# Context attention with its heads in two row halves, a pair of maxima per slot, and values weighed every second slot

## The reference, cut to what matters

```python
# ctx_512: 4 x 4096 x 128; HEADS = 16, D_K = 16
qh = (layernorm(x) @ Wq + bq)   # 4 batches x 16 heads x 256 queries x 16
kh = (ctx_512 @ Wk + bk)        # 4 batches x 16 heads x 4096 keys x 16
vh = (ctx_512 @ Wv + bv)
scores = einsum('bhqd,bhkd->bhqk', qh, kh) / 4
out = softmax(scores) @ vh
x = x + out @ Wo + bo
```

## Time and profile before

| | |
|---|---|
| times of three runs | 1427.91, 1429.73, 1433.0 us; median 1429.73 |
| span of the profiled execution | 1429.1 us, 0.6 below the median; no time around the span is shown |
| slot 0 begins, last slot begins | 67.1 us, 963 us |
| busy share PE, DVE, ACT, POOL | 96%, 74%, 65%, 20% |
| mean granted clock of PE | 0.989; 1.00 in all of the slots |

### The profile page before, as it was taken

How to read it: one execution, slowest core, us unless ns; L and a number is a source line. 1 busy time by engine, 2 the same in 40 slices (tenths; PEclk the granted TensorE clock), 3 DMA queues, 4 the chain that set the end, 5 groups by cost and what they waited for, 6 DMA issues and landing times.

```text
span 1429.1 us, 28070 instructions
## 1 busy us (share of the span) xinstructions
PE 1375.6 (96%) x11138; PEld 846.7 (59%) x11138; DVE 1055.1 (74%) x2114; ACT 922.1 (65%) x1899; POOL 287.6 (20%) x321
## 2 busy tenths in 40 slices
PE   7799999999999999999999999999999999989998
PEld 5355555555555545555554556556557999856666
DVE  4787777787777778777778888835876778767757
ACT  5366777767777767777767666672796664448731
POOL 3354222222222222122213100000003100001210
PEclk9899999999999999999999999999999999999999
DMA  6966555346554545655454743002402320347000
GB/s 184 163 145 143 119 118 111 77 102 130 116 127 92 102 84 125 128 115 113 81 97 101 184 73 61 2 1 60 119 18 65 112 67 1 91 112 155 2 1 30
DMA packets 95587, 133.19 MB, mean 93 GB/s; under 512 B 8864, under 2 KB 70944, under 8 KB 89504
## 3 DMA queue, kind: packets, MB, share of 16 engines
q1 hardware_dynamic: 95456, 131.40, 42.3%
HBM read 94.15 MB, written 37.22 MB: 92 GB/s over the span
## 4 chain that ended last, share of the span: by engine, by line
PE 79%; ACT 8%; DVE 8%; DMA 2%; issue 2%; SPq 1%; POOL 0%; DVEq 0%; ACTq 0%
PE psum L559 16%; PE psum L540 13%; PE psum L524 13%; ACT probs L783 4%; PE psum L2132 4%; PE psum L587 3%; PE psum L2106 3%; DVE peaks L685 3%; PE psum L626 3%; PE psum L1226 2%; PE psum L2851 2%; PE psum L1623 1%; PE psum L275 1%; PE psum L2861 1%; PE psum L2814 1%
## 5 line engine op out<-in xcount | busy, mean ns | idle before, releaser
L685 DVE TENSOR_REDUCE peaks<-psum 128x1 f32<-128x512 f32 x1024 | 643.3, 684 | 197.0 <-PE psum L524 196.4
L783 ACT ACTIVATE probs<-psum 128x512 f32<-128x512 f32 x1024 | 529.0, 615 | 83.3 <-PE psum L540 79.4
L524 PE MATMUL psum<-keysT,queriesT 96*128 96x512 bf16 x1024 | 390.1, 384 | 13.2 <-DMA keysT<-key_parts 7.9
L540 PE MATMUL psum<-queriesT,keysT 98*128 98x256 bf16 x2048 | 392.4, 274 | 6.1 <-ACT queriesT L846 2.4
L540 PEld LDWEIGHTS psum<-queriesT,keysT 98*128 98x128 bf16 x2048 | 176.3, 99 | 191.7 <-ACT probs L783 72.1
L559 PE MATMUL psum<-probs,values 128*17 128x256 f32 x4096 | 245.9, 380 | 0.0
L559 PEld LDWEIGHTS psum<-probs,values 128*17 128x17 f32 x4096 | 107.2, 97 | 102.6 <-issue 27.1
L524 PEld LDWEIGHTS psum<-keysT,queriesT 96*128 96x128 bf16 x1024 | 98.6, 96 | 90.9 <-issue 56.1
L918 POOL CAST key_parts<-key_f 128x512 bf16<-128x512 f32 x57 | 34.8, 611 | 518.0 <-ACT key_f L816 511.0
L816 ACT ACTIVATE key_f<-psum,bk 128x512 f32<-128x512 f32 x59 | 40.5, 687 | 120.7 <-PE psum L587 120.6
L587 PE MATMUL psum<-ctxT,wk 128*128 128x512 f32 x128 | 69.5, 625 | 2.4 <-DVE probs L728 0.9
(11 more groups left out here) (315 smaller groups left out, 1662.5 us busy)
## 6 DMA issues: line engine op xcount, KB each, us to landing
keysT<-key_parts SPq DMA_DIRECT2D x31, 768.0 KB, 7.7
key_parts<-key_parts SPq DMA_DIRECT2D x90, 256.0 KB
keysT<-key_parts SPq DMA_DIRECT2D x31, 512.0 KB, 10.1
ctx_nat<-in_ctx_dram SPq DMA_DIRECT2D x32, 256.0 KB, 3.0
keysT<-key_parts SPq DMA_DIRECT2D x31, 256.0 KB, 11.6
ctx_in<-in_ctx_dram SPq DMA_DIRECT2D x24, 256.0 KB, 5.9
ctx_turned<-ctxT SPq DMA_DIRECT2D x24, 256.0 KB, 4.4
ctx_T<-ctx_turned SPq DMA_DIRECT2D x12, 512.0 KB, 3.8
```

What stands on the lines that cost most here:

```text
L524: e.matmul(ps, self.queriesT[0:ROWS, u % 2, g * GH + j, t * P:(t + 1) * P], self.keysT[0:ROWS, i % RING, j, c * BANK:(c + 1) * BANK], star ...
L540: made = e.matmul(ps[:, j * S:(j + 1) * S], self.keysT[0:AUG, i % RING, j, kt * P:(kt + 1) * P], self.queriesT[0:AUG, u % 2, g * GH + j, : ...
L685: e.tensor_reduce(self.peaks[:, i % 2, pair, c:c + 1], k.ps(("max", n)), AX.X, ALU.max).then_inc(*self.peaked.up(n))
L783: e.activation(self.probs[:, t % RINGP, e2 * GH * S:(e2 + 1) * GH * S], k.ps(("scores", t, e2)), ACT.Exp).then_inc(*self.exped.up((t, e2)))
```

## The change

Three things change, all in the first block.

1. The two heads of a group stand in two row halves of the array: head 0 in partitions 0 to 63, head 1 in 64 to 127. `keysT` and `queriesT` get two planes: `MAIN` with four of the six products (64 rows), and `REST` with the other two and the two rows of the maximum (34 rows). A score is two matmuls in a row, one of each plane, that add up; a slot has eight of 256 columns instead of four. Each head has a bank for the whole slot, shared by both key tiles, so ACT's exponentials are one for each head and not one for each key tile. The maxima are taken over the four products of `MAIN` alone, one matmul for each head, and both stand behind the slot's scores.
2. The values are weighed every second slot (`BLOCK` = 2), after the maxima.
3. Value projections of a batch come every eighth slot (the last four more closely), and the jobs on even slots, the weighings on odd ones.

With it go six DMAs instead of three where keys are read (of 32 partitions each, the same bytes), four instead of three for query rows, five instead of three for a batch's query parts, and two copies of the maximum's rows on ACT instead of one.

```diff
-HALVES, SUMS = 3, 3
+SCORES, SUMS, BLOCK = (0, 1, 2), 3, 2
...
-        self.keysT = sb(scope, "keysT", [P, RING, GH, LC], BF16)
+        self.keysT = sb(scope, "keysT", [P, 2, RING, LC], BF16)
...
-                slot = UNIT * u - 101 + 8 * c
+                slot = UNIT * u - 100 + 8 * c
...
-                at(SLOTS * NG * b - 97 + 6 * p, "make values", b, p)
+                at(SLOTS * NG * b + (8 * p - 96 if p < 12 else (-6, 0, 2, 8)[p - 12]), "make values", b, p)
...
-            e.matmul(ps, self.queriesT[0:ROWS, u % 2, g * GH + j, t * P:(t + 1) * P],
-                     self.keysT[0:ROWS, i % RING, j, c * BANK:(c + 1) * BANK],
-                     start=True, stop=True).then_inc(*self.max_made.up(n))
+            e.matmul(ps, self.queriesT[own, MAIN, u % 2, g, qt * P:(qt + 1) * P],
+                     self.keysT[own, MAIN, i % RING, c * BANK:(c + 1) * BANK],
+                     start=True, stop=True).then_inc(*self.max_made[j].up(n))
...
-            for e2 in range(2):
-                if 0 <= t < TOTAL:
-                    kt, n = 2 * p + e2, (2 * t + e2) % HALVES
-                    ps = banks.use(n, w, ("scores", t, e2), (self.exped, (t, e2)))
-                    for j in range(GH):
-                        made = e.matmul(ps[:, j * S:(j + 1) * S], self.keysT[0:AUG, i % RING, j, kt * P:(kt + 1) * P],
-                                        self.queriesT[0:AUG, u % 2, g * GH + j, :], start=True, stop=True)
-                    made.then_inc(*self.scored.up((t, e2)))
-                if maxima and not e2:
-                    find_max(maxima[0], t)
-            if t % 4 == 1 and 5 <= t <= TOTAL + 1:
-                i, p0 = divmod(t - 5, SLOTS)
+                ps = {}
+                for e2 in range(2):
+                    kt = 2 * p + e2
+                    for plane, rows in ((MAIN, HALF), (REST, TALL)):
+                        for j in range(GH):
+                            if j not in ps:
+                                ps[j] = banks.use(SCORES[(2 * t + j) % len(SCORES)], w, ("scores", t, j), (self.exped, (t, j)))
+                            own = slice(j * HALF, j * HALF + rows)
+                            made = e.matmul(ps[j][:, e2 * S:(e2 + 1) * S], self.keysT[own, plane, i % RING, kt * P:(kt + 1) * P],
+                                            self.queriesT[own, plane, u % 2, g, :], start=(plane == MAIN), stop=(plane == REST))
+                            if e2 and plane == REST:
+                                made.then_inc(*self.scored[j].up((t, j)))
+            for n in maxima:
+                find_max(n, t)
+            if (t - 1) % BLOCK == 0 and BLOCK + 1 <= t <= TOTAL + 1:
+                i, p0 = divmod(t - BLOCK - 1, SLOTS)
...
-            for n in maxima[1:]:
-                find_max(n, t)
...
-                for e2 in range(2):
-                    w.wait_ge(self.scored, (t, e2))
-                    e.activation(self.probs[:, t % RINGP, e2 * GH * S:(e2 + 1) * GH * S], k.ps(("scores", t, e2)),
-                                 ACT.Exp).then_inc(*self.exped.up((t, e2)))
+                for j in range(GH):
+                    w.wait_ge(self.scored[j], (t, j))
+                    e.activation(self.probs[:, t % RINGP, 2 * j * S:(2 * j + 2) * S], k.ps(("scores", t, j)),
+                                 ACT.Exp).then_inc(*self.exped.up((t, j)))
...
-        for block, run in RUNS:
-            e.dma_start(self.keysT[block * DH:(block + run) * DH, i % RING, :, keys],
-                        self.key_dram[u, g * GH:(g + 1) * GH, PARTS - run:PARTS, :, keys].rearrange(
-                            "j i d n -> (i d) j n")).then_inc(*landed.up(key))
+        for j in range(GH):
+            for row, plane, first in ((0, MAIN, 1), (LOW, MAIN, 1), (0, REST, 0)):
+                e.dma_start(self.keysT[j * HALF + row:j * HALF + row + LOW, plane, i % RING, keys],
+                            self.key_dram[u, g * GH + j, first:first + 2, :, keys].rearrange("i d n -> (i d) n")).then_inc(
+                    *landed.up(key))
```

More of the change, by code:

```diff
@@ L297 @@
 RUNS = ((0, 3), (3, 2), (5, 1))
-PAIRS = 6
-ROWS = PAIRS * DH
-AUG = ROWS + 2
+KEY_AT = (1, 2, 0)
+QUERY_AT = ((2, 3), (0, 1), (4,))
+HALF = P // 2
+MAIN, REST = 0, 1
+LOW = 2 * DH
+TALL = LOW + 2
 NG = H // GH
@@ L512, in find_max @@
         def find_max(n, now):
-            i, r = divmod(n, MAXES)
-            pair, c = self.max_at(n)
-            j, t = divmod(pair, QT)
+            i, j, qt, c = self.max_at(n)
             u, g = divmod(i, UNIT_GROUPS)
+            own = slice(j * HALF, (j + 1) * HALF)
             job, let_go = ("max", n), (self.peaked, n)
@@ L978, in sync @@
                     n, first, last = CONST_COLS["ones"]
-                    for r in range(ROWS, AUG):
-                        e.dma_start(self.keysT[r:r + 1, :, :, :].rearrange("o r h n -> o (r h n)").bitcast(F32).rearrange(
-                            "o (p n) -> o p n", p=P), io["const"][:, first:last].unsqueeze(0)).then_inc(*self.ones_in.up(0))
+                    for r in (LOW, LOW + 1, HALF + LOW, HALF + LOW + 1):
+                        e.dma_start(self.keysT[r:r + 1, REST, :, :].rearrange("o r n -> o (r n)").bitcast(F32).rearrange(
+                            "o (p n) -> o p n", p=P), io["const"][:, first:(first + last) // 2].unsqueeze(0)).then_inc(
+                            *self.ones_in.up(0))
                 elif job == "load x":
@@ L989, in sync @@
                     if i >= RING:
-                        w.wait_ge(self.scored, (SLOTS * (i - RING + 1) - 1, 1))
+                        for j in range(GH):
+                            w.wait_ge(self.scored[j], (SLOTS * (i - RING + 1) - 1, j))
                     self.read_keys(e, i, slice(0, LC), self.keys_here[i % RING], i)
@@ L1002, in sync @@
                     if u >= 2:
-                        w.wait_ge(self.scored, (UNIT * (u - 1) - 1, 1))
-                    for block, run in RUNS:
-                        e.dma_start(self.queriesT[block * DH:(block + run) * DH, u % 2, :, :],
-                                    self.q_dram[b, :, 0:run, :, m, :].rearrange("h i d n -> (i d) h n")).then_inc(
-                            *self.rows_here[u % 2].up(u))
+                        for j in range(GH):
+                            w.wait_ge(self.scored[j], (UNIT * (u - 1) - 1, j))
+                    for plane, rows, parts in ((MAIN, HALF, slice(0, 4)), (REST, LOW, slice(3, 5))):
+                        for j in range(GH):
+                            e.dma_start(self.queriesT[j * HALF:j * HALF + rows, plane, u % 2, :, :],
+                                        self.q_dram[b, j::GH, parts, :, m, :].rearrange("h i d n -> (i d) h n")).then_inc(
+                                *self.rows_here[u % 2].up(u))
                 elif job == "load output weights":
```

57 lines of the change are left out of this document (31 added, 26 removed).

## The result

The changed kernel takes 1436.14 us (median of 20 runs, 1428.93 to 1438.66). The kernel before, run as often beside it, takes 1433.04 (1426.95 to 1435.17). The ratio is 1.0028 [1.0016, 1.004]: the change costs 3.1 us, which is inside the 0.3% that the text above calls no change. The profiled execution spans 1434.0 us, 4.9 more than that of before.

A forecast was written before the change was run, and what follows sets the result against it. PE was taken as the bound. The second batch went 221.0 - 28.2 + 7.0 + 11.6 + 12.0 - 6 + 1 = 218.4; slots +5 and prologue +1 gave +6 on 1429.1, 1435.1, plus 0.6 for the median: 1436 us, range 1423 to 1449.

The forecast's parts named there:

- no change: Whole kernel: a time between 1425.4 and 1434.0 us, 0.3%, about what a measurement tells from no change; chance 0.21.
- slower: Whole kernel: a time slower than the 0.3% band that ends at 1434.0 us; chance 0.48.
- Maxima, -28.2 a batch: PE, every slot: two maxima of 0.22 us in turn become two side by side, -28.2 us over 128 slots.
- the rival of halves that don't overlap: PE scores and maxima: bf16 row halves take turns, 0.66 us more in 512 slots, 1717 us; chance 0.05.
- Turns at 0.09, first weights at 0.10: PE at jobs: each change of array shape costs 0.09 us, fp32 first weights in the open 0.10; +11.6 a batch.
- The stand after an empty slot, 0.60, some 20 times: PE after even slots without a job: waits 0.60 us for head 0's exponential, 20 such slots, +12.0 in the second batch.
- empty slots cost little: PE after even slots without a job: the 93 stands of 0.6 us halve (1408 us) or vanish (1379); chance 0.24.
- Weighing +7: PE weighing values: 64 visits a batch instead of 32, same rounds, 32 x 0.22 = +7.0 us.
- waits of now -6: PE in the second batch: of 8 us of waits in the kernel before, 2 are left, -6 us.
- The batches: Slots by batch: first about 0, second and third -2.6 us each, last +10; together +5.
- Prologue: Before the slots: six more key reads issued by SP, 2.6 us, some of it hidden, +1 us.
- More waits: Row maxima's and key copies ahead of exponentials: 0.5 us for each of 32 groups, 3 of prologue, 1455 us; chance 0.2.

The follow-up runs named there:

- the pair of experiments: Changed kernel with a 16-column matmul before the maxima of 246 odd slots: over 128 rows (two turns of shape) 1477.44 us, over 64 rows (none) 1437.1 us.
- The fillers: Changed kernel with each maximum made three times: in 71 even slots without a job 1436.85 us, in slots with a value or key projection 1468.5 us.
- the fourth bank: Changed kernel with four score banks instead of three, leaving three instead of four for maxima and jobs: 1444.13 us, ratio 1.0105.
- the halved value projections: Changed kernel with values of batches 1 to 3 projected one key tile at a time, each half in an even slot: 1420.97 us, ratio 0.9924.
- maxima ahead: Changed kernel with the two maxima of odd slots placed ahead of the slot's scores: 1434.26 us, ratio 1.0014.

## Why the prediction was nearly right, point by point

**The time.** 1436 was forecast and 1436.14 measured, but part of that is luck: the forecast was +6 us on 1429.73, and the 20 runs of before have 1433.04, so the change costs 3.1 (2.3 to 5.7 by the interval). In the profiled executions the last slot begins 6.0 later, as in the sum, and what follows is 1.0 shorter, for +4.9 in all. The forecast lay at 0.4% slower and the result at 0.28%, on the other side of the bound between slower and no change, so "slower" had a larger chance (0.48) than the traces bear out.

**Maxima, -28.2 a batch.** Right: two side by side in 0.38 us drawn. That each half streams bf16 at full pace with its weight loads behind it is right as well, so the rival of halves that don't overlap falls. A sentence of the Trainium skill ("TensorE: Matmul & The Clock Gate", Part 3) lets loads overlap only where row groups differ; the trace does not agree, here as before: eight scores start and end within 0.62 us, though the loads of each half go to the rows on which its last matmul runs. The same part also lets a load run ahead into a background weight buffer, and by that the trace would be as it is.

**Turns at 0.09, first weights at 0.10.** Right: a turn is 0.08 to 0.09 by the pair of experiments, and the four matmuls of a value projection are drawn 1.13 long where they were 1.03. The forecast slots of 1.75, 1.39 and (0.66 + 0.87 + 0.29) 1.82 are 1.76, 1.36 and 1.83. The Trainium skill's rule that changing the tiling mode drains the engine ("TensorEngine Tiling (Array Packing)", Key Properties) agrees with the trace: behind the last of a pair of maxima, whose columns take 0.22, no matmul of the full array starts before 0.30; before, behind a maximum of 96 rows, the first of a turn of context or a value projection started after 0.22.

**The stand after an empty slot, 0.60, some 20 times.** Right in place and number, a little small: 0.63 or 0.69. The exponential begins 0.65 or 0.71 after the slot's start and not 0.60, with 0.65 from there to PE's next matmul (0.66 forecast). The 0.60 came from a misread row. I took the exponential at 419.26 for the one of the scores that end there (418.88 + 0.38), but ACT was behind:

```profile
418.79 1.08 ACT L783 ACTIVATE probs<-psum 128x512 f32<-128x512 f32 x2
```

Its exponentials follow each other 0.48 apart here, and the one at 419.26 is that of the key tile before, whose last score ends at 418.82; that of the scores ending at 419.26 begins at 419.74. That the two times fall together is chance. Where ACT is idle, the kernel before has the same 0.04 and 0.10 behind the scores as the changed one. The fillers show that it is latency (0.44 us are free in an empty slot and cost 0.44 in another), the fourth bank that it is the bank, and the halved value projections that it can be filled. The forecast's 12.0 us a batch should have been 13.4, and this is what the second batch lacks (218.4 forecast, 219.6 measured). The rival "empty slots cost little" needed under 0.5 and falls.

**Weighing +7, waits of now -6.** Each is about right in size, but they are one thing and not two. I took the waits of before as a remainder that goes with other costs; the kernel before with `BLOCK` = 2 alone shows that the visits themselves remove them, at no net cost. Had I known that, I'd have seen that this part is neutral by itself, and needed in the changed kernel: with four slots between weighings it takes 1485.0. One wait I called hidden is not: before a group's first slot ACT makes the two copies of the row maximum, 0.40 apart, ahead of the exponential that PE's second score needs, and that score comes 0.3 late, eight times, 2.4 us a batch.

**The batches.** Second and third: -2.6 forecast, -1.4 measured. First: 0 forecast, -2.4. Last: +10 and +11.0, with 29 waits of PE for exponentials where 28 were forecast. Prologue: +1 and +0.2, which says nothing, since it differs by up to 4.4 us between executions of the same code. What made the first batch's miss was not tried. "More waits" had the right place in the copies, but they cost 0.3 a group and not 0.5, about what the kernel before paid for its one copy (PEld waits 3.4 us for them in the batch, and 3.9 before), and the rest of it did not come.

**Where the gain went.** In the second batch maxima side by side give 28.2 us. Turns and first weights of the jobs take 11.6, weighings 7, stands 13.4, copies 2.4; to come to the measured gain of 1.4, 7.6 must have come back from waits. This is a remainder, and near the 8 us of waits that the forecast found in the kernel before. (Over all four batches the forecast's parts add to 25 us of waits given back, not the 27 of its closing sentence; the total of +6 goes by the 25.) The stands alone are a matter of where jobs lie, and splitting a job that was there anyway got some 14 us back in the whole kernel.

## What to carry to other kernels

When two streams share one engine side by side, add up what their shape costs at every switch (here 0.08 to 0.09 us each) before counting the columns saved. And when a stage becomes shorter than the way round to the engine behind it and back (here 1.30 to 1.36 us from scores to the next scores that need the bank), the place of the remaining jobs decides: cut them in pieces of the size of the hole and spread them, and look which buffer is next before taking one away, because both cures that shortened the wait for ACT (a fourth bank, maxima ahead) met DVE's next. A cost and a wait that lie on the same engine must not be added as if independent: remove one alone in the old kernel, and see.

## What was unexpected of the hardware

Matmuls in different row halves start out of the program's order: a maximum of half 1 at 408.80 before a score of half 0 at 408.90 that stands ahead of it, and a half held up by 0.22 us doesn't hold the other. A change of shape costs 0.08 to 0.09 us, on both sides of a matmul of 16 columns that itself puts the next one off by 0.03. An instruction of ACT that waits for one signal begins 0.04 us after the drawn end of the matmul that gives it, and 0.10 after it where the wait is an instruction of its own because there is a second signal to wait for, in both kernels; here this is 0.06 us of PE's time at 13 of 20 stands.
